# A first turn in another order, loads in another order, and y + bo behind the probabilities in every turn

## The reference

```python
# layer 0: 8 heads of 32; heads 0 to 5 have static masks, 6 and 7 have adj or the diagonal
q, k, v = (split_heads(x @ W.T + b) for W, b in ((Wq, bq), (Wk, bk), (Wv, bv)))
scores = where(mask, einsum('bhsd,bhtd->bhst', q, k) * SCALE, -1e9)
out = einsum('bhst,bhtd->bhsd', softmax(scores), v)          # then heads joined
x = layernorm(x + out @ Wo.T + bo)
# layer 1: 4 heads of 256
Wh = einsum('bni,hoi->bhno', h, W) + bW
e = einsum('bhno,hop->bhnp', Wh, attn)
A = tanh(where(adj, einsum('bhnp,bhmp->bhnm', e, Wh), 0))
hp = relu(einsum('bhnm,bhmo->bhno', A, Wh))
ha = cat(hp) @ A_w.T;  hf = h @ fc_w.T
coeff = sigmoid(hf @ g1_w.T + ha @ g2_w.T + gbias)
x = layernorm(x + hf * coeff + ha * (1 - coeff))
```

## Time and profile before

| | us |
|---|---|
| median of 3 runs | 1247.8 (1244.65 to 1253.7) |
| the profiled execution | 1256.22 |
| its span, first to last instruction | 1254.4 |
| first turn, up to the first T product | 81.55 |
| PE busy, DVE busy, ACT busy, POOL busy | 1156.9, 723.7, 511.4, 240.9 |
| mean granted clock of PE | 0.966 |

### The profile page before, as it was taken

One profiled execution on the slowest core, in us unless ns is written; L12 is line 12 of the kernel. 1 busy time (PEld: TensorE's weight loads), 2 busy tenths in 40 slices (PEclk: granted clock), 3 DMA queues, 4 the chain that ended last, 5 costly groups with the idle time before them and its releaser, 6 DMA issues.

```text
span 1254.4 us, 24543 instructions
## 1 busy us (share of the span) xinstructions
PE 1156.9 (92%) x9756; PEld 939.7 (75%) x9756; DVE 723.7 (58%) x1321; ACT 511.4 (41%) x910; POOL 240.9 (19%) x230
## 2 busy tenths in 40 slices
PE   5789989999899999989999998999999899998886
PEld 5667868788786878878687787878778787877765
DVE  6345565656556575655657565565756556574533
ACT  3535343443534344353534435343443534344241
POOL 1321121312112131212213121121312122130100
PEclk8789999999999999999999999999999999998898
DMA  6000001010000101000010100001010000100000
GB/s 210 20 19 20 19 18 38 17 37 17 19 18 17 37 17 37 17 19 18 17 37 17 36 17 19 18 17 37 17 37 17 19 18 17 37 18 2 1 17 17
DMA packets 26699, 32.58 MB, mean 26 GB/s; under 512 B 4400, under 2 KB 23344, under 8 KB 26288
## 3 DMA queue, kind: packets, MB, share of 16 engines
q1 hardware_dynamic: 26672, 32.19, 7.8%
HBM read 23.80 MB, written 8.39 MB: 26 GB/s over the span
## 4 chain that ended last, share of the span: by engine, by line
PE 87%; issue 4%; DVE 4%; ACT 3%; SPq 0%; DMA 0%; POOL 0%; POOLq 0%; DVEq 0%; ACTq 0%
PE bankB L329 18%; PE bankB L330 17%; PE bankB L331 17%; PE bankB L508 6%; PE bankA L329 5%; PE bankB L524 5%; PE bankA L330 5%; PE bankA L331 5%; PE bankA L424 3%; PE bankA L449 2%; ACT U_hi L725 1%; PE bankB L570 1%; PE bankA L475 1%; PE bankA L435 1%; ACT PT L686 1%
## 5 line engine op out<-in xcount | busy, mean ns | idle before, releaser
L731 ACT ACTIVATE cat_hi<-bankB 128x512 fp32r<-128x512 f32 x128 | 76.5, 598 | 134.7 <-PE bankB L331 134.7
L801 DVE SCALAR_TENSOR_TENSOR cat_lo<-bankB,cat_hi 128x512 fp32r<-128x512 f32 x128 | 86.4, 685 | 55.1 <-ACT cat_hi L731 54.1
L801 DVE SCALAR_TENSOR_TENSOR U_lo<-bankB,U_hi 128x512 fp32r<-128x512 f32 x128 | 79.5, 683 | 63.0 <-ACT U_hi L725 63.0
L329 PE MATMUL bankB<-hT_lo,g_hi 128*128 128x512 f32 x256 | 108.7, 425 | 0.0
L703 ACT ACTIVATE T<-bankB 128x512 f32<-128x512 f32 x128 | 75.4, 589 | 78.2 <-PE bankB L331 78.2
L329 PE MATMUL bankB<-U_lo,wt_hi 128*128 128x512 f32 x256 | 102.9, 402 | 3.7 <-DVE U_lo L801 2.3
L330 PE MATMUL bankB<-U_hi,wt_lo 128*128 128x512 f32 x256 | 101.4, 396 | 0.0
L331 PE MATMUL bankB<-U_hi,wt_hi 128*128 128x512 f32 x256 | 101.3, 396 | 0.0
L330 PE MATMUL bankB<-hT_hi,g_lo 128*128 128x512 f32 x256 | 101.0, 394 | 0.0
L331 PE MATMUL bankB<-hT_hi,g_hi 128*128 128x512 f32 x256 | 100.1, 391 | 0.0
L329 PE MATMUL bankB<-cat_lo,aw_hi 128*128 128x512 f32 x256 | 99.6, 389 | 0.0
(11 more groups left out here) (141 smaller groups left out, 2663.7 us busy)
## 6 DMA issues: line engine op xcount, KB each, us to landing
x_raw<-in_xT SPq DMA_DIRECT2D x16, 512.0 KB, 3.3
y<-in_x SPq DMA_DIRECT2D x16, 512.0 KB, 3.6
out<-res SPq DMA_DIRECT2D x16, 512.0 KB, 3.0
W_nat<-in_Wn SPq DMA_DIRECT2D x1, 1028.0 KB, 5.9
adjS_u<-in_adjS SPq DMA_DIRECT2D x32, 32.0 KB, 2.8
attn_nat<-in_attn SPq DMA_DIRECT2D x1, 1024.0 KB, 8.0
raw_A<-in_AwT SPq DMA_DIRECT2D x1, 1024.0 KB, 10.0
adjT_u<-in_adjT SPq DMA_DIRECT2D x16, 32.0 KB, 2.8
```

The costliest lines, as they stand in the source:

```text
L329: pe.matmul(out, asel(a[0]), bsel(b[1]), start=first, stop=False)
L731: act.activation(cat_hi[:, n, :], bank[:], ACT.Relu).then_inc(cat_hi_ready, 1)
L801: return dve.scalar_tensor_tensor(out=out, in0=bank, scalar=bias, in1=hi.bitcast(F32), op0=op, op1=ALU.subtract)
```

## The change

It has five parts.

1. Loads: W, v's weight and attn are issued ahead of the masks, bias_v, adjS, the diagonal (eye2) and the identity. The seven constants had one semaphore; now there are four, and ACT's q copies wait for all three biases.
2. First turn: M1's first two products stand ahead of the scores, the rest between the halves of values; G's products are spread over the transposed probabilities, values and attention, with their copies on ACT and DVE; DVE shifts W ahead of wv_lo and the mask; `new_h(0)` stands ahead of the gate weights on DVE; queries of group 1 stand ahead of h_T(0) on PE; POOL's `late` stands behind `root_1`.
3. Every turn: on POOL y + bo stands behind the four scalings of the probabilities.
4. Every turn: on ACT the exponentials stand behind T4, T5, T7 and the first hf copy, in place of T3, T4, T5 and T6; on PE and ACT the second half of hf stands ahead of attention, the first half of values between the halves of the gather, and the other half behind all four transposes.
5. The bank tables follow. hT has the banks of the keys, in place of those of the queries.

```diff
 SCORES_FROM = 1
+EXP_AFTER = (4, 5, 7)
 SETUP = 22
-          "probT0": 2, "probT1": 3, "probT2": 0, "probT3": 1, "attn00": 2, "attn01": 3, "attn10": 0, "attn11": 1,
-          "y0": 2, "y1": 3, "hT0": 0, "hT1": 1}
+          "probT0": 1, "probT1": 2, "probT2": 3, "probT3": 0, "v1": 1, "attn00": 2, "attn01": 3, "attn10": 0, "attn11": 1,
+          "y0": 2, "y1": 3, "hT0": 2, "hT1": 3}
...
             load(raw_k[:], wk, early_in[1])
-            for dst, src in ((bias_q, bq), (bias_k, bk), (bias_v, bv), (ident, eye)):
-                load(dst[:], src, const_in)
-            load(raw_m[:], masks, const_in)
+            load(bias_q[:], bq, bias_in)
+            load(bias_k[:], bk, bias_in)
+            load(W_nat[:], Wn, nat_in)
+            load(raw_v[:], wv, early_in[2])
+            load(attn_nat[:], attn, attn_in)
+            load(raw_m[:], masks, mask_in)
+            load(bias_v[:], bv, bias_in)
+            adjS_load(0)
             for half_ in range(2):
-                load(eye2[half_ * S:half_ * S + S], eye[0:S, 0:S], const_in)
-            load(raw_v[:], wv, early_in[2])
-            adjS_load(0)
-            load(W_nat[:], Wn, nat_in)
-            load(attn_nat[:], attn, attn_in)
+                load(eye2[half_ * S:half_ * S + S], eye[0:S, 0:S], eye_in)
+            load(ident[:], eye, ident_in)
...
             def turn(A, B, more):
                 if B is None:
-                    qk(0)
+                    queries(0)
+                    keys(0)
+                    M1_products(range(2))
                     for two in (0, 2):
                         scores(0, range(two, two + 2), range(NG))
-                    values(0)
-                    M1_products()
-                    probs_T(0, range(JB))
+                    values(0, 0)
+                    M1_products(range(2, H2 * DC))
+                    probs_T(0, range(2))
+                    G_products(range(4))
+                    probs_T(0, range(2, JB))
+                    values(0, 1)
+                    G_products(range(4, 5))
                     attention(0)
-                    G_products()
+                    G_products(range(5, H2 * DC))
                     project(0)
                     W_transposed()
                     gate_weights()
+                    queries(1)
                     h_T(0)
-                    qk(1)
+                    keys(1)
                     return
...
-                h_fc(B)
+                h_fc(B, 0)
                 adj_scores(B)
-                if A is not None:
-                    values(A)
-                for q2 in range(2):
-                    gathered(B, q2)
-                    if A is not None:
-                        probs_T(A, range(2 * q2, 2 * q2 + 2))
+                gathered(B, 0)
+                if A is not None:
+                    values(A, 0)
+                gathered(B, 1)
+                if A is not None:
+                    probs_T(A, range(JB))
+                    values(A, 1)
+                h_fc(B, 1)
                 if A is not None:
                     attention(A)
...
+            def queries(g):
+                if not later(g):
+                    act.wait_ge(bias_in, 16 * 3)
...
                 for n in range(KC):
                     T_out(B, n)
-                    if A is not None and 0 <= n - SCORES_FROM - 2 < JB:
-                        exps(A, n - SCORES_FROM - 2)
-                h_fc(B)
+                    if A is not None and n in EXP_AFTER:
+                        exps(A, EXP_AFTER.index(n))
+                h_fc(B, 0)
+                if A is not None:
+                    exps(A, JB - 1)
                 adj_tanh(B)
...
             def turn(A, B, more):
                 if B is None:
                     mask(0)
+                    x_and_bias(0)
                     probs_scaled(0)
-                    late()
                     x_low(1)
                     root_1(0)
+                    late()
                     mask(1)
                     hT_whole(0)
                     return
...
                 if A is not None:
                     probs_scaled(A)
+                    x_and_bias(A)
```

More of the change, by code:

```diff
@@ L401, in values, with keys @@
-            def values(g):
+                if not later(g):
+                    pe.wait_ge(weights_ready, 1)
+                for c in range(DC):
+                    bank = claim(pe, "A", f"q{c}", g)
+                    filled(dense(bank[:], [
+                        (Wq, (x_hi, x_lo), lambda t, k=k: t[:, k, c * P:c * P + P], lambda t, k=k: t[:, k, :])
+                        for k in range(DC)]), "A", f"q{c}")
+            def keys(g):
+                if not later(g):
+                    pe.wait_ge(weights_ready, 2)
+                for c in range(DC):
+                    bank = claim(pe, "A", f"k{c}", g)
+                    filled(dense(bank[:], [
+                        (Wk, (x_hi, x_lo), lambda t, k=k: t[:, k, c * P:c * P + P], lambda t, k=k: t[:, k, :])
+                        for k in range(DC)]), "A", f"k{c}")
@@ L402, in values @@
+            def values(g, t2):
                 if not later(g):
                     pe.wait_ge(weights_ready, 3)
[L404 to L411, removed]
+                bank = claim(pe, "A", f"v{t2}", g)
+                for q in range(2):
+                    p = 2 * t2 + q
+                    ins = dense(bank[:, q * D:q * D + D], [
+                        ((x_hi, x_lo), Wv, lambda t, k=k: tile_cols(t[:, k, :], p), lambda t, k=k: t[:, k, :])
+                        for k in range(DC)])
+                filled(ins, "A", f"v{t2}")
@@ L430, in probs_T @@
             def probs_T(g, js):
+                if not later(g) and 0 in js:
+                    pe.wait_ge(ident_in, 16)
                 for j in js:
@@ L489, in T_tile, with h_fc @@
                     for k in range(DC)]), "B", f"T{n}")
-            def h_fc(g):
-                for c in range(DC):
-                    bank = claim(pe, "B", f"hf{c}", g)
-                    filled(dense(bank[:], [
-                        (FF, (hT_hi, hT_lo), lambda t, k=k: t[:, k, c * P:c * P + P], lambda t, k=k: even_first(t[:, k, :]))
-                        for k in range(DC)]), "B", f"hf{c}")
+            def h_fc(g, c):
+                if c == 0 and not later(g):
+                    pe.wait_ge(ff_ready, 1)
+                bank = claim(pe, "B", f"hf{c}", g)
+                filled(dense(bank[:], [
+                    (FF, (hT_hi, hT_lo), lambda t, k=k: t[:, k, c * P:c * P + P], lambda t, k=k: even_first(t[:, k, :]))
+                    for k in range(DC)]), "B", f"hf{c}")
             def adj_scores(g):
@@ L539, in h_a @@
             def h_a(g):
+                if not later(g):
+                    pe.wait_ge(late_ready, 2)
                 for c in range(DC):
@@ L754, in turn @@
                     early()
[L755 to L759 removed]
+                    queries(0)
+                    masks_in()
+                    keys(0)
+                    M1_copies(range(2))
+                    exps(0, 0)
+                    values(0, 0)
+                    M1_copies(range(2, 3))
+                    exps(0, 1)
+                    M1_copies(range(3, 6))
+                    exps(0, 2)
+                    M1_copies(range(6, H2 * DC))
+                    out_weight()
+                    exps(0, 3)
+                    probs_T(0, range(2))
+                    G_high(range(4))
+                    probs_T(0, range(2, JB))
+                    values(0, 1)
+                    G_high(range(4, 5))
+                    attention(0)
+                    G_high(range(5, H2 * DC))
                     late()
[L761 to L763 removed]
                     x_split(1)
```

135 lines of the change are left out of this document (65 added, 70 removed), and 1 row of the table B_BANK.

## The result

| | before | changed | ratio |
|---|---|---|---|
| median | 1250.19 us (1244.65 to 1253.7, 4 runs) | 1184.77 us (1183.68 to 1185.59, 4 runs) | 0.948, 95% 0.944 to 0.952 |
| profiled execution | 1256.22 | 1183.68 | |
| its span | 1254.4 | 1181.9 | |
| mean granted clock of PE | 0.966 | 0.992 | |

The changed kernel is 5.2% faster; 1193 (1160 to 1214) was forecast. Between the medians lie 65.4 us, between the profiled executions 72.5.

What follows compares the result with a forecast made beforehand. TensorE, busy 92% of 1254.4 us, was taken as the bound, except where it waits or runs at its lower clock. Gains of 15 + 38 + 1.4 = 54 us took 1256.2 to 1202; less 8.4 for the median, 1193 us (1160 to 1214).

Steps and rivals of the forecast that it cites:

- wait before L521, its time: Adjacency products (L508 before the change), steady turns: the 1.97 us wait goes; 3.67 us, never 5.36.
- steady interval, unhindered: Attention to attention without a mask conflict: 73.51 - 3.6 (waits) - 0.9 (low clock) = 69.0 us.
- price of mask 2's hold: y + bo starts some 0.1 us before mask 2 and delays U_lo and second gather: 1.8 us a turn, bounds 0 and 3.1.
- W ready, softmax start: First turn: W's shift ends at 13 to 15 us, not 18.27; first softmax starts near 17.3, against 18.2.
- project's end, first T product: First turn: project ends at 46 us (42.5 to 50.5), not 60.0; T starts near 66.8, against 81.55.
- first turn: First turn's gain, chiefly from PE's order: 15 us, bounds 8 and 24.
- second turn (first T product to attention): Second turn: its own waits, 1.35 us at attention and 0.5 in the gather, pay for its mask conflict: 0.
- from the last attention to the end: Last turn: no POOL work meets the masks, and hf1 fills PE's wait for U_lo: 1.4 us gained.
- lock costs nothing: Rival: mask 2 gets in ahead of y + bo in steady turns, 27 us more gained: 1166 us; chance 0.33.
- POOL keeps the pair through two instructions: Rival: PE waits 3.1 us before each turn's first gather; total between 1213 and 1238 us; chance 0.12.
- its first sentence on the steady turns: y + bo goes behind the probabilities' scaling: norm L988 loses 2.06 us and softmax starts that much earlier.
- late's hold: First turn: POOL's late (L1049, 4.55 us) holds h's tensor_scalar on DVE; the tail is 21.5 us, 15 without it.

Runs made afterwards that it cites:

- the two halves: Changed kernel with y + bo as two POOL instructions of half the size, at the same place: 1169.6 us, ratio 0.937.

## Why the prediction was right, point by point

The verdict and the mechanism of the hold were right; each gain in the sum was forecast smaller than it measured. That 1193 lies within 9 us of 1184.8 owes something to luck: the measured terms, taken as the prediction took its own from its median of before, would give 1247.8 - 72.4 = 1175.

| step | forecast | measured |
|---|---|---|
| norm beside POOL, then without | 3.44, 1.38 us | 3.44, 1.38 us |
| wait before L521, its time | none, 3.67 us | none, 3.67 us |
| steady interval, unhindered | 69.0 us | 68.76 (y + bo behind the masks, 14 intervals, 96.01 to 1058.62) |
| price of mask 2's hold | 1.8 us a turn | 70.18 - 68.76 = 1.42 |
| steady interval | 70.8 | 70.18 |
| W ready, softmax start | 13 to 15, 17.3 | 13.94, 18.45 |
| project's end, first T product | 46, 66.8 | 44.3, 65.56 |
| first turn | 15 us | 16.0 |
| second turn (first T product to attention) | 0 | 0.7 |
| 14 intervals | 38 us | 14 x 3.33 = 46.6 |
| from the last attention to the end | 1.4 us | 112.0 - 102.9 = 9.1 |
| sum | 54 us | 72.4 |

- **Steady turns.** The chain was right: L988's hold goes, mask 1 gets in between two scalings, y + bo wins against mask 2. The forecast had 0.1 us between those two, and the trace has 0.17, on the same side, in each of the 13 turns. A sum of terms good to a few tenths could not settle 0.1 us, so the side was in part luck. The rival "lock costs nothing" was thus a near one; its time, 1166 us, is what the kernel takes when the conflict is removed (1163.2). The rival "POOL keeps the pair through two instructions" is refuted by mask 1, which is never held through a second instruction of POOL, and by the two halves. (Its times were 1213 to 1238 us, of which only the last few lie within 1% of before, not half, as the prediction has it.) What was mis-sized is the term of the interval, by 0.62 us: 0.24 in the unhindered turn and 0.38 in the hold. The forecast passed U_lo's whole delay on to PE. U_lo was 1.62 us late, and PE waited 1.23, with 0.3 more in the gather's longer 2.33.
- **Credit to the parts.** The prediction led the end of the wait before L508 back to the norm's hold and to T7's copy leaving the exponentials together, and did not part them. The runs do: with the hold back and the new order the kernel takes 1181.3 us. The order on ACT and PE had made the softmax's start unimportant. The forecast was right for the change as a whole; its first sentence on the steady turns names a cause that would have been enough in the old order and carries nothing in the new.
- **First turn.** W, bias_v's wait and late's hold came as forecast. The softmax starts 1.15 us later than forecast, but PE waits 0.9 us for the probabilities instead of 2.7, and its granted clock is 1.00 from 14.4 to 44.3 us, where I had charged 1.5. h took 6.54 us, its first instruction held by L1100 to 55.03, its second by late's next one to 56.29, and the stretch from project's end to the first T product took 21.3 us for a forecast 20.8.
- **The end** is the term that failed most, 9.1 for 1.4. In 41.32 us from the last paired attention to the transpose L570 of the trace before lies a wait of 1.97 us within attention and a stretch at 1.2 GHz behind it; after, the same path takes 36.69 with neither. Of the remaining 4.5 us 1.4 are hf1, as forecast. The rest goes with low clock behind the waits of the last turn: the granted clock is 0.78 in 1183.6 to 1195 and 0.88 from there to the end, against 0.85 and 0.93 in the same stretches of after. Each side has one trace for this. I had looked for clock losses in the steady turn only.
- **Profile against median.** That the sum came out larger for the profiled pair (72.4) is partly that execution's own: it was 6.0 us above the median of before, the changed kernel's 1.1 below its own. Between medians the gain is 65.4. The runs of the kernel before spread over 9 us, those of the changed kernel over 2; which waits and clocks make that spread isn't shown, since only one execution of before has a trace.

The Trainium skill, SBUF — State Buffer, section SBUF: two separate sides, has the rule on which forecast and repair rest: an exclusive lock for a whole instruction. The traces agree at five places: norm (3.44 for 1.38 us), mask 2 (2.75 for 0.69), the gate's product (2.75 for 0.69), h (6.54 for 1.38) and, with POOL as the loser, the fourth scaling (1.5 for 1.04). Norm and h don't have the two SBUF inputs by which the prediction named the rule: one tensor is their input. That they are held is measured; by what they take the lock, no run shows. What stays open is the wait without a releaser in the attention of the first turn: 2.24 us in the changed kernel, 2.0 to 2.5 in seven of its variants, 1.6 the longest with M1 and G in one block, none in the one with the old loads. No run was made to tell why.

## What to carry to other kernels

List the instructions of two engines that exclude one another, and place the pairs by what waits behind them. A hold costs only where the held instruction is the next thing someone needs: 2 us were worth 1.4 at one place and nothing at another. When an edit is credited with a gain, undo it alone in the final kernel as well as doing it alone in the first: y + bo's move was worth 36 us in the old order and -3.5 in the new. Splitting the long instruction of such a pair is the cheap repair, a wait in the program the full one.

## What was not expected of the hardware

- At the boundary between two instructions of POOL that follow one another, the waiting DVE instruction gets the access. With y + bo moved back, mask 1 asked at 225.89 while the third scaling ran (to 226.22), and took 0.88 us; with y + bo in halves, mask 2 went in between them. The waiting POOL instruction then took 0.4 to 0.6 us longer. In the changed kernel's steady turns mask 1 shows nothing of this, since it asked before the fourth scaling.
- How late a held instruction ends goes by its kind: the masks and the gate's product, 0.69 us alone, ended 0.54 to 0.55 us behind POOL's instruction; norm and h, 0.41 us alone, 0.15 behind it.
- The prediction used it already, and the runs bear it out beside y + bo: a DVE instruction with one input in PSUM kept its own length (U_lo, 2.48 us for four beside y + bo's 2.40), while a tensor_scalar from SBUF to SBUF (norm, h), with one tensor as its input, was held too.
- PE stands still for about 2 us within the attention products, 128 short instructions in a row, with no releaser shown: 1.97 us in the last paired turn of before, 2.24 in the first turn of after. Most traces have it in one turn or two, the one with y + bo moved alone in three (1.6, 1.7 and 1.4 us).
